# First routed head: two norms per chunk take their inverse roots by Newton steps on VectorE

## The reference, cut to what matters

```python
x = x_q + o @ Wo.T                                    # attention output, already there
h = gelu(layer_norm(x, g1, be1) @ W1.T + b1)          # 128 -> 512
x = x + h @ W2.T + b2
y = layer_norm(x, g2, be2)                            # the second norm (mean, variance, rsqrt(var + 1e-5))
X = X + tanh(gate) * y                                # the model's residual

xf = layernorm(X)                                     # (X - mean) / sqrt(var + 1e-5): the route norm
logits = clip(xf @ Wr)                                # 8 experts, top 2 of them per token
...                                                   # slots per expert in the order of the tokens, experts, sum back
```

## Time and profile before

| what | value |
|---|---|
| device time, median of 3 runs | 1389.69 us (1388.54 to 1392.05) |
| device time of the profiled execution | 1398.8 us |
| its span, first to last instruction | 1396.8 us |
| mean granted TensorE clock | 0.878 |
| busy: TensorE, VectorE, ScalarE, GpSimd | 1114.7, 702.7, 616.6, 454.4 us |
| head of the stage, first GELU feed-forward output (L1743) to the last scatter | 198.2 to 265.0 us |
| first instruction of the experts' loop on TensorE | 269.94 us |

### The profile page before, as it was taken

How to read it: one execution, slowest core, us unless ns; L and a number is a source line. 1 busy time by engine, 2 the same in 40 slices (tenths; PEclk the granted TensorE clock), 3 DMA queues, 4 the chain that set the end, 5 groups by cost and what they waited for, 6 DMA issues and landing times. The chain is left out here.

```text
span 1396.8 us, 26596 instructions
## 1 busy us (share of the span) xinstructions
PE 1114.7 (80%) x8678; PEld 764.2 (55%) x8678; DVE 702.7 (50%) x3353; ACT 616.6 (44%) x1537; POOL 454.4 (33%) x645
## 2 busy tenths in 40 slices
PE   5997965399989999979998766997577999951793
PEld 3675844287854666664344654787453444441573
DVE  4563657133367777644453454111767888664002
ACT  3443543133358766624212331333473666620453
POOL 1673634433314545510001545344010000016343
PEclk8998988599999999999997885799695999975797
DMA  7499230222029990001740003464231222050443
GB/s 207 126 282 225 60 106 31 69 78 86 17 80 124 123 172 2 1 28 33 151 86 16 3 17 104 135 174 127 60 113 61 59 71 57 19 148 23 111 114 95
DMA packets 148022, 125.39 MB, mean 90 GB/s; under 512 B 14025, under 2 KB 124505, under 8 KB 147896
## 3 DMA queue, kind: packets, MB, share of 16 engines
q1 hardware_dynamic: 133016, 104.53, 32.2%
q0 software_dynamic: 7824, 15.47, 4.2%
q10 hardware_dynamic: 7056, 3.81, 1.0%
HBM read 88.91 MB, written 37.70 MB: 91 GB/s over the span
## 5 line engine op out<-in xcount | busy, mean ns | idle before, releaser
L938 ACT ACTIVATE L_Z<-L_Z,L_nmx 128x154 f32<-128x154 f32 x256 | 105.1, 414 | 42.3 <-DVE L_nmx L988 42.2
L3158 DVE CUSTOM_DVE_ANT_0 L3s_masked<-L3s_psS,L3s_trilw 128x512 f32<-128x512 f32 (+3 forms) x256 | 109.1, 487 | 28.6 <-PE L3s_psS L3057 28.1
L324 POOL TENSOR_TENSOR L_Z<-L_Z,L_mx 128x512 f32<-128x512 f32 x84 | 88.5, 1054 | 103.3 <-DVE L_mx L674 103.3
L3129 ACT ACTIVATE L3s_E<-L3s_psT 128x512 f32<-128x512 f32 (+1 forms) x192 | 87.7, 531 | 48.5 <-PE L3s_psT L3070 48.3
L807 POOL TENSOR_TENSOR L_Z<-L_Z,L_rin 128x488 f32<-128x488 f32 x64 | 64.0, 1000 | 110.8 <-DVE L_rin L996 110.8
L674 DVE CUSTOM_DVE_ANT_0 L_Z<-L_psS,L_Z 128x154 f32<-128x154 f32 x256 | 63.4, 313 | 59.6 <-PE L_psS L379 49.8
L849 PE MATMUL L_psS<-L1k_G,L_xnT 128*128 128x462 f32 x192 | 82.4, 525 | 3.0 <-DVE L_nmx L988 1.6
L988 DVE CUSTOM_DVE_ANT_0 L_Z<-L_psS,L_mask 128x154 f32<-128x154 f32 x256 | 67.7, 312 | 11.5 <-PE L_psS L849 10.3
L555 ACT ACTIVATE L_E<-L_psT 128x512 f32<-128x512 f32 x84 | 46.5, 596 | 61.1 <-PE L_psT L392 58.9
L1006 DVE COPY L_PT<-L_psT 122x512 f32<-122x512 f32 x64 | 43.6, 681 | 40.1 <-PE L_psT L859 39.3
L2291 DVE TENSOR_TENSOR L0f_h<-L0f_h,L0f_psB 128x384 f32<-128x384 f32 (+1 forms) x64 | 31.2, 488 | 64.2 <-PE L0f_psB L2253 51.8
(11 more groups left out here) (555 smaller groups left out, 2848.4 us busy)
## 6 DMA issues: line engine op xcount, KB each, us to landing
L_Z<-in_fside_Bx16xSxS SPq DMA_DIRECT2D x16, 1232.0 KB, 9.6
L2f_w<-in_L_ffn_W SPq DMA_DIRECT2D x39, 256.0 KB
slotsL<-empty SPq DMA_DIRECT2D x1, 8320.5 KB, 75.7
L1m_cb<-comb_rows SPq DMA_DIRECT2D x8, 1024.0 KB
L3f_w<-in_L_ffn_fc_w SPq DMA_DIRECT2D x32, 256.0 KB
L0f_w<-in_L_ffn_W SPq DMA_DIRECT2D x24, 256.0 KB
L3s_QS<-q_parts SPq DMA_DIRECT2D x144, 32.0 KB
L3s_KS<-k_parts SPq DMA_DIRECT2D x48, 96.0 KB
```

Source lines behind the costliest of these rows:

```text
L324: nc.gpsimd.tensor_tensor(Z[:, t % NZ, h, 0:KM_], Z[:, t % NZ, h, 0:KM_], top.broadcast_to([P, HG, KM_]), ALU.subtract).then_inc(z_ready, 1)
L938: last = nc.scalar.activation(Z[:, t % 2, h], Z[:, t % 2, h], ACT.Exp, scale=-1.0, bias=nmx[:, t % 2, h:h + 1], accum_out=sums[:, t % 2, h ...
L3129: nc.scalar.activation(E[:, g.par, h, EO[group[0]]:EO[group[0]] + wd], psT[:, k, 0:wd], ACT.Exp).then_inc(t_free, 1)
L3158: last = nc.vector.tensor_tensor_reduce(masked[:, k, at:at + wd], psS[:, k, at:at + wd], trilw[:, S - wd:S], 1.0, LOW, ALU.add, ALU.max, m ...
```

## The change

Both small square roots of each chunk leave ScalarE, with their waits, and both reciprocals leave VectorE. In their place VectorE runs `newton_root`: half of the negated variance, the variance plus 1e-5, a first guess from the bits of the float as an integer, and three Newton steps of three instructions. These are 12 instructions on 128x4 operands; the first two don't depend on each other, each later one waits for the one before it. The square root at L1688, over all 16 tiles, stays. The second and fourth routed heads keep their ScalarE roots (`Route.deviation` and `Route.apply` stay for them).

```diff
+ROOT = float(0x5f3759df)
...
+def newton_root(nc, own, var, y, tmp):
+
+    ve, half, t = tmp
+    dve = nc.vector
+
+    def step(ins):
+        own.done(ins)
+        own.wait()
+
+    own.done(dve.tensor_scalar(half, var, -0.5, -0.5 * EPS, ALU.mult, ALU.add))
+    step(dve.tensor_scalar(ve, var, 1.0, EPS, ALU.mult, ALU.add))
+    step(dve.tensor_scalar(y.bitcast(I32), ve.bitcast(I32), -0.5, ROOT, ALU.mult, ALU.add))
+    for _ in range(3):
+        step(dve.tensor_tensor(t, y, y, ALU.mult))
+        step(dve.tensor_tensor(t, t, half, ALU.mult))
+        step(dve.scalar_tensor_tensor(y, t, 1.5, y, ALU.add, ALU.mult))
...
-        def deviation2(k):
-            ts = slice(k * TB, (k + 1) * TB)
-            act.wait_ge(self.var2_ready, k + 1)
-            nc.scalar.activation(self.std[:, ts], self.mv[:, ts, 1], ACT.Sqrt, bias=m.const["eps"]).then_inc(self.std2_ready, 1)
-
         turned1(0)
         for k in range(TB):
             gelus(k, 0)
...
             gelus(k, 1)
             if k >= 2:
                 route.turned_copies(act, k - 2)
-            if k >= 1:
-                deviation2(k - 1)
             if k + 1 < TB:
                 turned1(k + 1)
-            if k >= 1:
-                route.deviation(act, k - 1)
-        deviation2(3)
         route.turned_rows(act, 2)
         route.turned_copies(act, 2)
-        route.deviation(act, 3)
         route.turned_rows(act, 3)
         route.turned_copies(act, 3)
         route.exponentials(act)
...
         def second(k):
             ts = range(k * TB, (k + 1) * TB)
-            dve.wait_ge(self.std2_ready, k + 1)
-            own.done(nc.vector.reciprocal(self.rs[:, k * TB:(k + 1) * TB], self.std[:, k * TB:(k + 1) * TB]))
-            own.wait()
+            newton_root(nc, own, self.mv[:, ts[0]:ts[-1] + 1, 1], self.rs[:, ts[0]:ts[-1] + 1], [self.newton[:, n] for n in range(3)])
             dve.wait_ge(self.xb_ready, k + 1)
...
-            route.apply(k, m.X)
+            ks = slice(k * TB, (k + 1) * TB)
+            dve.wait_ge(route.var_ready, k + 1)
+            newton_root(nc, own, route.mv[:, ks, 1], route.rs[:, ks], [self.newton[:, n] for n in range(3)])
+            for t in range(k * TB, (k + 1) * TB):
+                last = nc.vector.tensor_scalar(self.pay[:, 0, t, 0:D], m.X[:, t], route.mv[:, t, 0:1], route.rs[:, t:t + 1],
+                                               ALU.subtract, ALU.mult)
+            last.then_inc(route.x_ready, 1)
```

More of the change, by code:

```diff
@@ L1603, in __init__ @@
         self.stats, self.mv = sb("stats2", [P, NT, 6]), sb("mv2", [P, NT, 2])
-        self.std, self.rs = sb("std2", [P, NT]), sb("rs2", [P, NT])
+        self.rs, self.newton = sb("rs2", [P, NT]), sb("newton", [P, 3, TB])
         self.f_in, self.std1_ready, self.x1_ready, self.t1_full, self.t1_done = (
@@ L1607, in __init__ @@
         self.h_full, self.h_free, self.o_full, self.o_free = (sem(s) for s in ("h_full", "h_free", "o_full", "o_free"))
-        self.gg_ready, self.xb_ready, self.var2_ready, self.std2_ready = (
-            sem(s) for s in ("gg_ready", "xb_ready", "var2_ready", "std2_ready"))
+        self.gg_ready, self.xb_ready, self.var2_ready = (sem(s) for s in ("gg_ready", "xb_ready", "var2_ready"))
         self.b2_ready = sem("b2_ready")
```

## The result

| what | before | after |
|---|---|---|
| device time, median of the timed runs | 1389.12 us (4 runs, 1387.49 to 1392.05) | 1401.34 us (4 runs, 1400.27 to 1404.51) |
| ratio, 95% interval | | 1.009 [1.007, 1.011] |
| device time of the profiled execution | 1398.8 us | 1401.19 us |
| its span; mean granted TensorE clock | 1396.8 us; 0.878 | 1399.0 us; 0.874 |

The kernel became slower by 12.2 us, or 0.9%. The forecast was +9.4 us. Note the profiled executions: they differ by 2.4 us only. The one of before stood 9 us over its median, so the two traces laid side by side would hide most of the result (the span, forecast at 1406.2 us from that trace, came out at 1399.0). I therefore give all places in the head as time since its first TensorE transpose (183.8 us in the trace before, 186.87 after), and add a second profiled execution of the unchanged kernel (run e8).

A forecast was written before the change was run, and what follows sets the result against it. VectorE was taken to bound the head: eight Newton roots at +2.07 us each and a fallen clock, less vanished waits and slack, make +9.4 us, 1389.7 + 9.4 = 1399.1 us; range 1394.2 to 1404.4 us.

The forecast's parts named there:

- The price of a root: VectorE in the head: 0.20 us a step, 2.28 us a Newton root, each of eight adding 2.07 us.
- The first scatter: GpSimd, chunk 0: slips by 3.1 us with `second(1)`, from 218.71 to 221.8 us.
- TensorE's idle time: Ahead of `route.turn(1)`: grows to 5.3 us, TensorE falls to half clock, `logits(1)` comes 1.8 us later.
- The rival in which the clock holds: TensorE ahead of `route.turn(1)`: no fall of the clock, only +7.6 us, 1397.3 us; chance 0.12.
- the credit for `place(1)`: VectorE's 3.11 us idle ahead of `place(1)` vanishes, since VectorE arrives 9 us later: slip falls to +6.0 us.
- the 0.94 us ahead of the reduction of chunk 2: VectorE's idle ahead of the reduction at 243.39 may vanish: `apply(3)` slips 10.4 to 11.3 us.
- The last slots: GpSimd, last eight scatters: 1.4 us of slack is used up, so they slip 9.0 to 9.9 us.
- ScalarE's release: Removed roots and loads gain chunk 0's waits (2.77 and 0.36 us) and 0.9 us at chunk 2's copy.
- The rival in which ScalarE sets the pace: ScalarE bounds the head: 8.8 us of loads and roots go, 1380.9 us; chance 0.03.
- the one in which the steps overlap: VectorE's dependent steps follow at 0.08 us, a root adds 0.75 us: 1387.4 us; chance 0.05.
- The scatters holding up the small steps: VectorE hand-overs late while GpSimd issues scatters: +6 us more, about 1405 us; chance 0.13.
- Something outside the head moves: 88 more instructions shift later VectorE code and its fetches: 5 us either way around no change; chance 0.10.

The follow-up runs named there:

- e8: The kernel before, unedited, profiled once more: 1387.74 us (one run), head 81.6 us.
- e3: Changed kernel plus 24 unused TensorE transposes between `hidden(3, 0)` and `route.turn(1)`: 1403.61 us, 1.0101 against the kernel before.
- e9: The changed kernel, unedited, once more on another chip: 1422.84 us, 1.0077 against the kernel before.
- e2: Changed kernel with ScalarE's `deviation2` and `route.deviation` put back at their old places, results unread: 1403.34 us, 1.0102 against the kernel before.
- e6: Changed kernel with Newton roots for the second norm only, the route norm back on ScalarE: 1397.43 us, 1.0055 against the kernel before.
- e11: Kernel before plus unused TensorE transposes in idle times and a Newton root for chunk 0's second norm only: 1410.81 us, 0.999 against the kernel before.
- e4: Changed kernel with no Newton step, only the first guess (inexact): 1390.17 us, 1.0007 against the kernel before.
- e1: Changed kernel with one Newton step instead of three (inexact): 1393.29 us, 1.0022 against the kernel before.
- e5: Changed kernel with six Newton steps instead of three: 1418.86 us, 1.0214 against the kernel before.
- e7: Kernel before plus unused TensorE transposes ahead of `route.turn(2)` and `(3)`, their positions and the experts: 1389.03 us, 0.9989 against the kernel before.
- e10: Changed kernel with 24 unused transposes ahead of `route.turn(1)`, again, on another chip: 1423.62 us, 1.0064 against the kernel before.

## Why the prediction was right, and where it was not

**The price of a root** was right: 0.195 to 0.20 us a step (predicted 0.20), 2.24 us a root (2.28), +2.05 each (+2.07). The two neighbours of the trace, the dependent and the independent pair on 128x8, gave both the price and the rule for which step gets which.

**The first scatter** slipped by 2.8 us (34.7 to 37.5; predicted 3.1). The sum had let all of `apply(0)`'s slip through to `choose(0)`; but VectorE had waited 0.58 us there for TensorE's logits and now waits 0.17, which takes up 0.4 us. **TensorE's idle time** ahead of `route.turn(1)` was 5.25 us (5.3) and brought the clock down. It fell while TensorE was still idle (granted 0.69 from 224 to 226 us, 0.50 from 226 to 227; the transposes start at 226.97), so `hidden` ran at half clock almost throughout, 3.62 us instead of the 3.37 that I had taken, and `choose(1)` waited 2.54 us (1.8; the two pairs of rows that the prediction names give 1.49 + 0.46 = 1.95 by themselves). It slipped by 7.2 us over e8 (predicted 7.0): 0.7 us more for the clock, 0.5 less for the rest. The rival in which the clock holds is refuted for this kernel, and e3 puts its price at 2.3 us.

**The step that failed** is the credit for `place(1)`: "Then VectorE stood idle for 3.11 us ahead of `place(1)` ... It now arrives 9 us later and should find it: +6.0." The idle time did vanish from the trace, as predicted, but not because of the change. It was a late hand-over that the first profiled execution had and e8 has not. The timed runs beside it, 1387.49 to 1392.05 us against its 1398.8, lie where e8 lies (1387.74), so in them the change had nothing to take away. In an execution that does have such waits the credit is real: e9, which has others of them, has none ahead of `place(1)`, and its head is 11.1 us longer than that of the first profile of before, of which 1.9 us are late Newton steps, so 9.2 (one profile of each). The sum without the credit is 9.4 + 3.1 = 12.5 us. Against e8 the head slips by 94.1 - 81.6 = 12.5 us, and the medians by 12.2. The same goes for the 0.94 us ahead of the reduction of chunk 2, which e8 doesn't have either; I had counted about half of it as vanished. Without either credit the list of the prediction gives 9.9 + 3.1 = 13.0 us for chunk 3's first scatter, and it slipped by 12.7.

The warning was in my own text. The profiled execution was 9.1 us over the median. I moved the sum from one to the other as if the difference lay elsewhere, but two "remote" waits (8.9 and 3.1 us) were in its list of waits, and the second was the one I credited.

**The last slots.** VectorE's slot numbers of chunk 3 slipped by 14.2 us over e8, and chunk 3's first scatter by 12.7. The 1.4 us of slack on GpSimd was used up, as predicted (14.2 - 12.7 = 1.5).

**ScalarE's release.** Costed at 0.9 us for the copy of chunk 2 and, behind chunk 0, at nothing elsewhere; e2 measures 0.8 us there and 1.2 in all. The waits of chunk 0, 2.98 and 0.57 us with their reciprocals, were credited in full. Up to the payload of chunk 0 that is right (it comes 0.9 us later, predicted 1.0), but e6 and e11 show that shortening this wait alone gains nothing: TensorE's logits hold VectorE next, behind the load back to GELU. That load was one of those costed at nothing; taking it away as well brings `choose(0)` 1.1 us forward (e4), where the Newton steps of the change use it up. The rival in which ScalarE sets the pace, 8.8 us to gain, is refuted by e4. So is the one in which the steps overlap.

**The scatters holding up the small steps** did not show in the profile after: all its Newton steps stand 0.19 to 0.21 us apart where scatters run. In e9 they did (VectorE in order of time):

```profile
247.89 0.17 DVE L1327 TENSOR_SCALAR L0f_newton<-L0f_mv 128x4 f32<-128x4 f32 x1
249.16 0.17 DVE L1328 TENSOR_SCALAR L0f_rs<-L0f_newton 128x4 int32<-128x4 int32 x1 [1.10 <-DVE L0f_newton L1327]
```

In all e9's Newton steps lose 1.9 us so. The same kernel had none of these in its first profile, and its ratio was no worse beside e9 (1.0077 against 1.009). Such late hand-overs are in profiles of both kernels; whether the changed one, with its 88 more hand-overs, pays more for them is not shown.

**Something outside the head moves.** It does, and one profile of each kernel can't settle by how much for this change: against e8 the profile after is 5.2 us longer ahead of the head, 12.5 in it and 4.5 shorter behind it. The series of experiments settles it better. In e1, e4, e6 and e5 the ratios make 3.1, 1.0, 7.6 and 29.8 us over the kernel before, and the heads are 2.7, 0.0, 6.4 and 28.5 us longer than in e8. The time follows the head, with 1.3 us at most left over.

## What to carry to other kernels

A chain of small dependent instructions is paid by the hand-over and not by the elements: count the steps, multiply by the start-to-start time of the nearest dependent pair in the trace, and compare that with the wait it removes, place by place; here it removed two waits, of 2.77 and 0.36 us, and was paid eight times. Before crediting an idle time of the profiled execution, ask whether the timed runs pay it: where the profiled time lies over their median and the wait has no producer that is late, take a second profile before counting on it. Removing a wait buys only as much as the next engine in line allows: TensorE's logits, behind a table load on ScalarE, took back all of the 0.8 us of chunk 0 (e6, e11), GpSimd's scatters 1.2 of the 2.2 us of e7.

## What was unexpected of the hardware

- Hand-overs between instructions of one engine, or from TensorE's finished count to VectorE, can be late by 0.5 to 1.1 us, and by 3.2 in the worst case of the head, without any work in between. All that I found in the head lie in the stretch in which GpSimd issues scatters, but scatters alone don't bring them: the profiles after, e1 to e8 have the same scatters and none of the long ones, the first one of before and those of e9, e10 and e11 have several, the longest one at the same place in two of them. What brings them stays open.
- An indirect DMA of 128 rows costs GpSimd 0.97 us and 0.30 of pause, 1.276 us in all, and this sets a floor under the head: 32 of them are 40.8 us.
- On one chip everything took 1.7% longer (1413.09 us for the kernel before) with the ratios in place. Only the ratio to the kernel before on the same chip is worth reading.
- TensorE's clock fell ahead of `route.turn` in idle times of 5.25, 4.86 and 6.15 us and of 3.74 us (e4, `route.turn(2)`, transposes of 1.09 us), and held in those of 2.63 (e3), 2.83 (e1) and 3.15 us (e6, transposes of 0.63 us). The length of the idle time alone doesn't decide it: ahead of e1's `route.turn(2)` it was 4.80 us, the grant was still 1.00 from 235 to 236, when the transposes began, and fell behind that (0.54 from 236 to 238). In the profile after, work began again at 226.97 and ran at 0.50 until 231 (0.93 in the next 4 us); in e5 it began at 214.89 and the grant was 0.68 from 217 to 218 and 1.00 behind that.
